# LoRA residual on one Trainium2 core: each 128-row output tile stored in two column halves instead of one whole tile

## The reference, cut to what matters

```python
def reference(x, itok_B_3_7, L0_cond_A, L0_cond_B):
    B_sel = B[adapter_ids]                       # (64, 16, 1024)
    A_sel = A[adapter_ids]                       # (64, 1024, 16)
    Bx = jnp.einsum('bni,bri->bnr', x, B_sel)
    out = jnp.einsum('bnr,bor->bno', Bx, A_sel)
    return x + out * SCALING                     # SCALING = 1.0
```

## Time and profile before

| | |
|---|---|
| median of 3 runs | 95.86 us (95.16 to 96.04) |
| the profiled execution, its own time | 95.48 us |
| span in the profile (first to last instruction) | 93.5 us |
| busiest engine | PE, 81.1 us (87% of the span) |
| bytes moved by DMA | 34.82 MB, mean 372 GB/s |
| packets of the queue that SP and its loads and stores use (q1) | 11040 |

### The profile page before, as it was taken

The page is one execution under the profiler, slowest core; times in us unless marked ns, Lnnn a source line. Parts: engine busy times, 40 slices in busy tenths (PEclk is TensorE's granted clock), DMA queues, the critical chain, the costliest instruction groups (busy, mean ns, idle before and its releaser), DMA issues.

```text
span 93.5 us, 3679 instructions
## 1 busy us (share of the span) xinstructions
PE 81.1 (87%) x1472; PEld 62.5 (67%) x1472; DVE 66.2 (71%) x121; ACT 53.3 (57%) x138; POOL 61.9 (66%) x136
## 2 busy tenths in 40 slices
PE   3992999999999899899999999999997999943910
PEld 3972898877878587677777686877775878611400
DVE  0009552057888968779889898989794989899960
ACT  1429777886767566567675757667673667430000
POOL 6004904999897949497979797979785979360000
PEclk9999999999999999999999999999999999999555
DMA  0899999999999999999999999999999999576596
GB/s 21 288 308 410 410 410 413 403 406 417 398 406 420 401 405 412 401 406 410 401 413 410 417 419 408 415 410 417 415 408 419 417 361 373 200 312 266 217 394 252
DMA packets 11202, 34.82 MB, mean 372 GB/s; under 512 B 2867, under 2 KB 2867, under 8 KB 11187
## 3 DMA queue, kind: packets, MB, share of 16 engines
q1 hardware_dynamic: 11040, 34.08, 92.3%
q10 hardware_dynamic: 146, 0.52, 1.5%
HBM read 17.83 MB, written 16.78 MB: 370 GB/s over the span
## 4 chain that ended last, share of the span: by engine, by line
PE 75%; DVE 12%; DMA 7%; issue 2%
PE t_bank L212 34%; PE bx_bank L225 20%; PE y_banks L245 18%; DMA x_all<-in_A 7%; DVE x_all L359 6%; PE y_banks L203 4%; DVE bx_parts L346 2%; DVE x_all L332 2%; DVE x_all L329 1%; DVE bx_parts L353 1%; DVE x_all L335 1%
## 5 line engine op out<-in xcount | busy, mean ns | idle before, releaser
L359 DVE TENSOR_TENSOR x_all<-y_banks,x_all 128x1024 f32<-128x1024 f32 x32 | 39.1, 1225 | 9.4 <-PE y_banks L245 8.8
L292 ACT COPY x_t<-t_bank 128x512 f32<-128x512 f32 x64 | 34.4, 590 | 19.7 <-PE t_bank L212 19.6
L160 POOL CAST a_duo<-a_table 128x512 fp32r x64 | 37.5, 627 | 5.3 <-ACT a_table L297 3.5
L212 PE MATMUL t_bank<-ident,x_all 128*128 128x128 f32 x256 | 35.0, 279 | 2.0 <-DMA x_all<-in_x 1.9
L150 POOL COPY b_duo<-b_table 128x256 f32 x64 | 23.5, 411 | 15.5 <-PE bx_bank L225 9.6
L212 PEld LDWEIGHTS t_bank<-ident,x_all 128*128 128x128 f32 x256 | 27.5, 141 | 8.5 <-issue 4.9
L245 PE MATMUL y_banks<-a_duo,bx_parts 64*128 64x512 f32 x128 | 20.7, 438 | 2.8 <-DVE bx_parts L353 2.3
L225 PE MATMUL bx_bank<-x_t,b_duo 128*32 128x64 f32 x1024 | 21.8, 222 | 1.6 <-issue 1.6
L225 PEld LDWEIGHTS bx_bank<-x_t,b_duo 128*32 128x32 f32 x1024 | 16.2, 109 | 7.6 <-issue 7.4
L346 DVE TENSOR_TENSOR bx_parts<-bx_bank,bx_parts 32x64 fp32r<-32x64 f32 x64 | 14.1, 220 | 4.8 <-ACT bx_parts L307 3.7
L245 PEld LDWEIGHTS y_banks<-a_duo,bx_parts 64*128 64x128 f32 x128 | 10.5, 192 | 7.7 <-DVE x_all L359 3.1
(11 more groups left out here) (13 smaller groups left out, 7.6 us busy)
## 6 DMA issues: line engine op xcount, KB each, us to landing
out_y<-x_all SPq DMA_DIRECT2D x32, 512.0 KB, 11.2
x_all<-in_x SPq DMA_DIRECT2D x15, 1024.0 KB, 18.8
x_all<-in_x SPq DMA_DIRECT2D x2, 512.0 KB, 6.9
x_all<-in_B ACTq DMA_DIRECT2D x1, 512.0 KB, 4.9
x_all<-in_A SPq DMA_DIRECT2D x1, 512.0 KB, 6.4
id_row<-in_ids ACTq DMA_DIRECT2D x1, 0.2 KB
```

What stands on the lines that cost most here:

```text
L160: last = nc.gpsimd.tensor_copy(a_duo[duo % 2][:, k, :], a_table[:, bass.ds(adapters[k] * BANK, BANK)])
L212: last = nc.tensor.transpose(t_bank[unit % 2][:, c * P:(c + 1) * P], x_all[:, 2 * duo + tile, at:at + P], ident[:, :])
L292: nc.scalar.copy(x_t[duo % 2][:, half * HALF:(half + 1) * HALF, tile, :], t_bank[unit % 2][:, :].rearrange("p (c n) -> p c n", c=HALF)).th ...
L359: nc.vector.tensor_tensor(here, y_banks[tile][:, :], here, ALU.add).then_inc(y_drained, 1)
```

## The change

The store of a tile is issued as two DMAs, one for each column half. Both follow the same wait for `y_drained`, the left half first. Each has 128 partitions by 2 KB (256 KB); in HBM its rows are 2 KB pieces at a distance of 4 KB. The last wait counts 64 transfers instead of 32.

```diff
             for tile in range(TILES):
                 sp.wait_ge(y_drained, tile + 1)
-                sp.dma_start(out_rows[:, tile, :], x_all[:, tile, :]).then_inc(stored, 16)
-            sp.wait_ge(stored, 16 * TILES)
+                for h in range(HALVES):
+                    cols = slice(h * BANK, (h + 1) * BANK)
+                    sp.dma_start(out_rows[:, tile, cols], x_all[:, tile, cols]).then_inc(stored, 16)
+            sp.wait_ge(stored, 16 * TILES * HALVES)
```

## The result

| | before | changed |
|---|---|---|
| median of 20 runs | 95.23 us (94.38 to 96.12) | 96.08 us (95.50 to 96.84) |
| the profiled execution, its own time | 95.48 us | 95.88 us |
| its span | 93.5 us | 94.1 us |

The ratio is 1.0096, with a 95% interval of 1.0074 to 1.0118. The change makes the kernel 0.9 us slower; the interval lies above 1, so the loss is clear of noise. The forecast was +0.13 us, "no change". Executions of this kernel fall into a faster and a slower state, and every ratio here compares runs of the faster one alone.

A forecast was written before the change was run, and what follows sets the result against it. It took TensorE's chain, ending in VectorE's last additions, to set the end, with 4.3 us of DMA idle as cover. Backlog 0 + last three tiles 0.13 + issues 0 + semaphores 0 = +0.13 us; forecast 95.8 us, range 95.0 to 96.9.

The forecast's parts named there:

- The packet's price: Store backlog: a 2 KB packet costs 82 ns, giving 400 GB/s and 0.042 us more a tile.
- The last three tiles: Last stretch of stores, with no cover: three tiles at 0.042 us make +0.13 us.
- The absolute forecast: Whole kernel: 95.8 us, put between 95.6 and a figure 0.4 above it; "no change", chance 0.80.
- the signs named for being right: 15,648 packets; 395 to 405 GB/s; later slack under 330; VectorE's additions unmoved; last landing 2.6 to 2.9 us after issue.
- The issues at 0: SP's store issues: 0.33 us each, two a tile, lying beside the transfers and adding 0 at the end.
- The cover of 4.3 us: Idle DMA time between 75 and 88.7 us, to absorb 1.2 us of slower backlog stores, leaving 3.1 idle.
- break-even of 370: Backlog from 47 us: above 370 GB/s the cover holds all; 0.148 us a tile more uses it up.
- its second way: Rate below which stores set the end: data end at 47.0 + 32 x the time of a tile.
- Rival A: Backlog from 47 us: 2 KB packets dear on the way to HBM; 97.7 us at 350 GB/s; chance 0.12.
- Rival B: Store queue: doubled issue or completion binds it; 0.25 us a transfer pair gives +3.7, 99.2 us; chance 0.03.
- Rival C: TensorE's 0.61 us pause at 70.16: shorter packets might halve it, -0.3 us, 95.3; over 1% faster, chance 0.05.

The follow-up runs named there:

- e4: Changed against the kernel before: tiles 0 to 27 stored two at a time by column half (512 KB transfers, 2 KB packets), last four whole; ratio 1.0143.
- e2: Changed against the kernel before: only tiles 29 to 31 stored in column halves, tiles 0 to 28 whole; ratio 0.9998.
- g4: Changed against the kernel before: whole-tile stores, at most three in flight for every tile; ratio 1.0043.
- f1: Changed against the kernel before: a second, redundant wait ahead of each store, 32 more SP instructions, no added packet or transfer; ratio 1.0081.
- h2: Repeat of f1 against the kernel before: 32 extra wait instructions on SP; ratio 1.0060.
- e1: The changed kernel but with tiles 29 to 31 stored whole, 61 transfers; ratio against the kernel before 1.0084.
- f2: The changed kernel but with tiles 0 to 7 stored whole and the rest in halves, 56 transfers; ratio against the kernel before 1.0077.
- e3: Changed against the kernel before: each tile stored in two transfers split by rows, 64 partitions of 4 KB each; ratio 1.0778.

## Why the prediction was wrong

**The packet's price: right.** Forecast 82 ns and 400 GB/s; e4 ran at 402, and the changed kernel at 400 until 56 us. The last three tiles were to cost 0.13 us, and e2 shows 0.2 between last addition and last landing and no change in the total.

**The absolute forecast: near by luck.** 95.8 us against 96.08 looks good only because it stood on a median of three runs, 95.86, while 20 runs of the kernel before gave 95.23. As a difference, +0.13 against +0.9 missed. Of the signs named for being right, only the packet count came: the rate was 379 and not 395 to 405, the slack from 80 to 85 us ran at 385 and not under 330, VectorE's last addition moved, and the last landing came 3.6 us after its first half's issue and not 2.6 to 2.9.

**The issues at 0: the step that failed.** The prediction took 0.33 us an issue, "between 0.17 and 0.44", from the median of an engine that was waiting for VectorE most of the time and from one single issue at the start. It named the right point, "SP would need more than 0.61 us an issue to become late", and the measured median is 0.645. SP was late: the last store left 1.02 and 1.20 us after the last addition in the two profiles, where the working had 0.38, and then needed 3.1 and 3.7 us to land, where the working makes 2.5 (93.14 + 0.13 - 90.79). In the kernel before the same instruction had mostly taken 1.05 to 1.24 us while the queue was full, which the row's maximum of 3105 ns hinted at; the median hid it. I had seen that issues would look longer and had put it down to a full queue. The backlog did stand in SP, as it says, but the queue didn't stay full: while SP issued, 256 KB in 1.1 us or more, the engines moved them in 0.66, and the queue emptied, to 3.4 us of issue to landing.

**The cover of 4.3 us: right in size, wrong in what draws on it.** Packets alone were to use 1.2 us of it. With the short queue the rate was 379 and 369 in two profiles, against a break-even of 370 that the prediction worked out (its second way, 47.0 + 32 x the time of a tile up to 92.7, gives 367). The sum had no term for an engine held by an instruction fetch while the other fifteen run dry. Nine hundred nanoseconds of one engine cost nothing with ten stores queued; with five they are a dip in the rate of all, and g4 shows the same with whole tiles.

**A term that was missing altogether: the 32 instructions.** The prediction counted the issues' time and not that the instructions must be fetched. f1 and h2, which add only these, lose 0.6 to 0.8%, most of what the change loses; e1, with 29 issues more and its last three stores whole, loses 0.8%.

**Rival A** (packets dear enough to bring the backlog to the end) named the right place and the right threshold; its cause was wrong, since the packets were not dear. **Rival B** (the doubled issue binds the queue) had the cause nearly right and got 0.03, on the argument that stores of 512 KB ran no slower than loads of 1 MB. That argument spoke of DMA engines; the thing that was doubled was SP's work. The sign it named, issues of more than 0.6 us in the last stretch, came in part: 0.33 to 1.04 us for the last five of the changed kernel, 0.33 to 0.67 in its second profile. **Rival C** (TensorE's pauses shrink when the stores hold up its instruction fetches less) was given -0.3 us. The pauses did shrink, by 1.1 us in the page's own group, and the one of 0.61 us that the prediction named is gone, though it goes with the depth of the queue and not the packet's size: e4 has 2 KB packets and a long queue, and the pauses grew. That such a pause is a held-up instruction fetch stays an inference.

The Trainium skill, "Perfetto Trace Analysis", DMA Optimizations, advises batching small transfers, 2 KB into 4 KB or 8 KB. Here the loss of rate by the packet's size alone was 414 to 402, 3%. Whether this does harm by itself isn't shown: e4 lost 1.4% and f2 0.8%, the first behind more pauses of TensorE, the second for a reason not found. The same page of the Trainium skill, section "What DMA-bound means", lists the issuing engine's sequencer as a second thing that can bind, seen as a solid row of DMA slices. The trace agrees: SP issues for 53.0 of the 57.6 us between its first store and its last.

**What stays open.** Of the +0.9 us I can show the parts (fewer pauses, 0.85 to 1.1 us at the last addition; from there to the last landing 1.4 to 2.2 us more) but not a fixed share for fetches in the tail and for the backlog: the two profiles of the changed kernel divide it differently. Why an issue of eight 2 KB packets an engine takes 1.2 us while the queue is long and 0.65 when it is short was not settled. Nor was why e3 is so slow, nor what f2 loses by, nor how much of the loss is SP's lateness and how much the trailing DMA engine: e1 has the second without the first.

## What to carry to other kernels

Before cutting a transfer in two, price the engine that issues it at the rate it has when it isn't waiting, and ask how deep the queue will be afterwards: a short queue lets every stall of one DMA engine through to all. Align profiles at the first addition before comparing where the last one ends: the start alone moved by up to 0.9 us between kernels that don't differ there. Depth works both ways, since a long store queue goes with pauses in an engine that fetches its instructions over the same DMA engines; where the trace shows such pauses ("issue" on the chain), try limiting the transfers in flight before touching their size. Instructions that do nothing are not free: here 32 cost 0.6 to 0.8%, probably because their fetch falls into the last microseconds.

## What the runs showed that I had not expected

- A limit of four stores in flight, which delays stores and lowers their rate from 414 to 390 GB/s, makes the kernel 0.6 to 0.9% faster, while TensorE's pauses fall from 1.6 to 0.7 us.
- 32 redundant waits on SP cost 0.6 to 0.8%.
- Stores of 64 partitions by 4 KB ran at 346 GB/s from 47 to 75 us and at 270 to 290 after it, where stores of 128 partitions by 2 KB, with the same bytes to a transfer, ran at 369 to 395 while they had work. (e3's profiled execution was 1.0 us over its median.)
- Behind one 16 KB instruction fetch the whole core's DMA share dipped to 0.78 in one microsecond, and in the second profile to 0.26, when the queue held some five transfers of 256 KB; with ten of 512 KB it stayed at 0.98 or more.
- An issue of 128 partitions took SP mostly 1.05 to 1.64 us with a long queue, whether the transfer had 512 or 256 KB, and 0.65 us with a short one. Halving transfers halves what SP can hand over in that time.
